# Order of the rounds in a gated delta-rule layer of a decoder kernel

## The reference

```python
q = jax.nn.silu(_dwconv_causal(x @ Wq, qconv_w, qconv_b))      # k and v in the same way
alpha, beta = jax.nn.sigmoid(x @ Wa + ba), jax.nn.sigmoid(x @ Wb + bb)
def step(S, inp):
    qt, kt, vt, at, bt = inp
    err = jnp.einsum('bhvk,bhk->bhv', S, kt) - vt
    S = at[..., None, None] * S - bt[..., None, None] * err[..., :, None] * kt[..., None, :]
    return (S, jnp.einsum('bhvk,bhk->bhv', S, qt))
_, outs = jax.lax.scan(step, S0, (qT, kT, vT, aT, bT))
o = (o - mu) * jax.lax.rsqrt(var + EPS) * ln_g + ln_b          # per head, over 128 values
o = (o * jax.nn.sigmoid(x @ Wg)).reshape(Bx, Lx, NH * DV)
return o @ Wo
...
x = _layernorm(x + _L0_attn_ref(x, ...), axis=-1)
```

## Time and profile before

| | us |
|---|---|
| median of three runs | 3799.28 (3796.48 to 3801.1) |
| the profiled execution | 3798.25 |
| its span in the profile | 3796.5 |
| PE busy, whole span | 3257.8 (86%) |
| DVE busy, whole span | 2811.0 (74%) |
| ACT busy, whole span | 1990.9 (52%) |
| POOL busy, whole span | 1132.7 (30%) |

### The profile page before, as it was taken

How to read it: one execution, slowest core, us unless ns; L and a number is a source line. 1 busy time by engine, 2 the same in 40 slices (tenths; PEclk the granted TensorE clock), 3 DMA queues, 4 the chain that set the end, 5 groups by cost and what they waited for, 6 DMA issues and landing times. The chain is left out here.

```text
span 3796.5 us, 63508 instructions
## 1 busy us (share of the span) xinstructions
PE 3257.8 (86%) x22659; PEld 2092.0 (55%) x22674; DVE 2811.0 (74%) x5796; ACT 1990.9 (52%) x4818; POOL 1132.7 (30%) x1191
## 2 busy tenths in 40 slices
PE   7899999998871777879899978789999999997775
PEld 3466666666551445655566645555666666664444
DVE  6888888886458675553477857769888898985768
ACT  5577777776632333321344425436666566663555
POOL 2633332264003000000011212106666565653210
PEclk9999999999995898889899979999999999997988
DMA  3433333332101100001000000312222222222000
GB/s 104 105 88 96 87 87 91 83 88 54 49 16 33 37 1 25 2 28 38 23 1 1 1 34 2 127 42 69 81 71 78 73 78 73 76 76 73 2 1 23
DMA packets 245463, 200.88 MB, mean 53 GB/s; under 512 B 114720, under 2 KB 213408, under 8 KB 244256
## 3 DMA queue, kind: packets, MB, share of 16 engines
q1 hardware_dynamic: 245152, 196.82, 17.5%
HBM read 181.39 MB, written 15.34 MB: 52 GB/s over the span
## 5 line engine op out<-in xcount | busy, mean ns | idle before, releaser
L310 PE MATMUL ps<-xT,min 128*128 128x512 f32 (+1 forms) x1072 | 496.1, 608 | 11.9 <-DVE macc L3475 11.4
L3475 DVE SCALAR_TENSOR_TENSOR macc<-ps,mcw,macc 128x508 f32<-128x508 f32 (+2 forms) x408 | 302.6, 742 | 80.0 <-ACT macc L3402 70.4
L3576 POOL TENSOR_TENSOR mSQ<-mSQ,mtn 128x512 f32<-128x512 f32 x128 | 234.9, 1835 | 331.1 <-ACT mtn L3427 331.0
L310 PEld LDWEIGHTS ps<-xT,min 128*128 128x128 f32 (+1 forms) x1072 | 191.0, 189 | 228.2 <-issue 205.7
L3569 POOL TENSOR_TENSOR mE<-mE,mCB 128x1024 f32<-128x1024 f32 x128 | 302.0, 2360 | 44.4 <-DVE mE L3485 26.4
L3485 DVE TENSOR_TENSOR_SCAN mE<-mE,mid 128x1024 f32<-128x1024 f32 x128 | 300.1, 2345 | 0.0
L3335 PE MATMUL ps<-mwo,macc 128*128 128x256 f32 x1024 | 243.0, 380 | 5.4 <-DVE macc L3492 5.4
L3080 DVE TENSOR_REDUCE hMX<-ps 128x2 f32<-128x512 f32 x256 | 165.4, 686 | 109.7 <-PE ps L2967 109.0
L3423 ACT ACTIVATE mtn<-ps,mcol 128x64 f32<-128x64 f32 x1024 | 222.1, 333 | 2.8 <-PE ps L3314 2.8
L3047 ACT ACTIVATE hE<-ps 128x512 f32<-128x512 f32 x256 | 138.9, 595 | 156.4 <-PE ps L2961 156.4
L2961 PE MATMUL ps<-hXE,hKE 32*128 32x256 f32 x1024 | 158.9, 428 | 54.8 <-DVE hMX L3080 40.7
(11 more groups left out here) (583 smaller groups left out, 8179.2 us busy)
## 6 DMA issues: line engine op xcount, KB each, us to landing
mE<-m_decay SPq DMA_DIRECT2D x128, 512.0 KB, 3.6
dE<-d_decay SPq DMA_DIRECT2D x64, 264.0 KB, 3.4
dwk<-in_L_attn_Wk SPq DMA_DIRECT2D x64, 128.0 KB, 2.3
dwq<-in_L_attn_Wq SPq DMA_DIRECT2D x64, 128.0 KB, 2.4
dwv<-in_L_attn_Wv SPq DMA_DIRECT2D x64, 128.0 KB, 2.3
dwg<-in_L_attn_Wg SPq DMA_DIRECT2D x64, 128.0 KB, 2.3
dwo<-in_L_attn_Wo SPq DMA_DIRECT2D x64, 128.0 KB, 2.3
min<-in_m_in SPq DMA_DIRECT2D x2, 4096.0 KB, 18.4
```

The lines of the kernel that those rows point to most:

```text
L310: t = pe.matmul(out, w[:, j, :], self.c.xT[:, j, blk(g, 512)], start=j == 0, stop=j == 1)
L3475: x = dve.scalar_tensor_tensor(out=acc[:, :, 3 - j:T], in0=p[:, :, 0:T - 3 + j], scalar=self.cw[:, i, j:j + 1], in1=acc[:, :, 3 - j:T], op ...
L3576: pool.tensor_tensor(self.SQ[g % 2][:, :], self.SQ[g % 2][:, :], self.tn[s][:, :], ALU.add).then_inc(*self.sqa.up)
```

## The change

Four things are changed in `order`, with what follows from them.

1. From round 64 on, v of unit w + 1 stands ahead of vt (behind p32) and no longer behind p64. In rounds up to 63 it keeps its place.
2. o stands directly behind gate, ahead of v1 and e, and oc, which was the first step of the next round, stands behind o in the same round.
3. acc is given unit x - 1 in place of x: each output projection comes one round later, and behind o. dGO becomes two tiles in turn, go waits for acc of unit u - 2, and SP loads the output weights one round later. close moves with acc.
4. The norm of a group, which was one step (stats) in the round after close, with scale in the second round after and turn in the third, becomes six rounds: close, then stat0 and stat1 (mean and variance of two sequences each), root0 and root1 (the root's first Newton step, then two more), scale, and turn behind it.

```diff
--- before.py
+++ after.py
@@ -61,6 +61,10 @@
 
 def blk(j, n=128):
     return slice(n * j, n * j + n)
+
+
+def blk2(j):
+    return 2 * j, 2 * j + 1
 
 
 class Core:
@@ -352,12 +356,12 @@
             for e in range(2):
                 sp.dma_start(self.bia[blk(g, 32), e:e + 1], i["d_abb"][blk(e, 32)]).then_inc(small, 16)
         sp.dma_start(self.small[:, :], i["d_small"]).then_inc(small, 16)
-        for t in range(-4, self.U + self.LAG + 4):
+        for t in range(-4, self.U + self.LAG + 5):
             if t == 0:
                 self.decays_out(sp)
                 for u in range(4):
                     self.decay_in(sp, u)
-            a, b, v, w, x = t + 4, t + 1 - self.LAG, t + 2 - self.LAG, t - 1 - self.LAG, t - 2 - self.LAG
+            a, b, v, w, x = t + 4, t + 1 - self.LAG, t + 2 - self.LAG, t - 1 - self.LAG, t - 3 - self.LAG
             if 0 <= a < self.U:
                 if a >= 4:
                     sp.wait_ge(*self.qp.at(a - 3))
@@ -453,7 +457,7 @@
         self.ak, self.aq, self.av = (c.f32("d" + n, 512) for n in ("ak", "aq", "av"))
         self.KQ, self.E, self.V, self.W = c.sets(2, "dKQ", 4, 2, 128), c.sets(4, "dE", 4, 132), c.f32("dV", 512), c.f32("dW", 512)
         self.seed = c.sets(2, "dsd", 4, 132)
-        self.G, self.O, self.L, self.GO = c.sets(2, "dG", 512), c.sets(3, "dO", 512), c.f32("dL", 512), c.f32("dGO", 512)
+        self.G, self.O, self.L, self.GO = c.sets(2, "dG", 512), c.sets(3, "dO", 512), c.f32("dL", 512), c.sets(2, "dGO", 512)
         self.TT, self.T, self.X, self.X2 = c.sets(4, "dTT", 512), c.sets(4, "dT", 4, 64), c.sets(2, "dX", 4, 32), c.sets(2, "dXX", 4, 64)
         self.s8, self.sw = c.sets(2, "dst", 8, 8), c.sets(2, "dsw", 24)
         self.NB, self.TB, self.TTB, self.tmp = c.sets(2, "dNB", 32, 32), c.f32("dTB", 32, 32), c.f32("dTTB", 32, 32), c.f32("dtmp", 256)
@@ -480,14 +484,16 @@
     def order(self):
 
 
-        for t in range(self.U + self.LAG + 8):
+        for t in range(self.U + self.LAG + 12):
             a, b, v, w, x = t, t - 1, t - self.LAG, t - self.LAG - 2, t - self.LAG - 5
-            every = (("oc", w - 1), ("k", a), ("st", w - 1), ("c1", w - 1), ("c2", w - 2), ("p32", v), ("k1", a), ("on", x), ("q", a), ("vt", w),
-                     ("cols", a), ("s0", b), ("s1", b), ("k2", a), ("p64", v - 1), ("q1", a), ("seed", a), ("v", w + 1), ("ot", x), ("v0", w + 1),
-                     ("go", x), ("w", w), ("q2", a), ("gate", x + 1), ("v1", w + 1), ("e", a), ("acc", x), ("v2", w + 1), ("o", w),
-                     ("close", x), ("stats", x - 1), ("scale", x - 2), ("turn", x - 3))
+            y, late = w + 1, t >= self.U
+            every = (("k", a), ("st", w - 1), ("c1", w - 1), ("c2", w - 2), ("p32", v), ("k1", a), ("on", x), ("q", a), *([("v", y)] * late),
+                     ("vt", w), ("cols", a), ("s0", b), ("s1", b), ("k2", a), ("p64", v - 1), ("q1", a), ("seed", a), *([("v", y)] * (not late)),
+                     ("ot", x), ("v0", y), ("go", x), ("w", w), ("q2", a), ("gate", x + 1), ("o", w), ("oc", w), ("v1", y), ("e", a),
+                     ("acc", x - 1), ("v2", y), ("close", x - 1), ("stat0", x - 2), ("stat1", x - 3), ("root0", x - 4), ("root1", x - 5),
+                     ("scale", x - 6), ("turn", x - 7))
             for step, u in every:
-                if step in ("close", "stats", "scale", "turn"):
+                if step in ("close", "stat0", "stat1", "root0", "root1", "scale", "turn"):
                     due = u % 16 == 15 and (step, u) != ("turn", self.U - 1)
                 elif step in ("c1", "c2"):
                     due = u % 2 == 1
@@ -624,7 +630,7 @@
                     for b in range(2):
                         pe.wait_ge(*room[b])
                 for j in range(4):
-                    t = pe.matmul(bank(j // 2)[:, blk(j % 2, 256)], self.GO[:, blk(j)], self.wo[u % 4][:, :],
+                    t = pe.matmul(bank(j // 2)[:, blk(j % 2, 256)], self.GO[s][:, blk(j)], self.wo[u % 4][:, :],
                                   start=h == 0 and j % 2 == 0, stop=h == 15 and j % 2 == 1, skip_group_check=True)
                 t.then_inc(*self.accd.up)
                 if h == 15:
@@ -831,9 +837,9 @@
             elif step == "go":
                 dve.wait_ge(*self.os.at(u + 1))
                 dve.wait_ge(*self.gt.at(u + 1))
-                if u:
-                    dve.wait_ge(*self.accd.at(u))
-                dve.scalar_tensor_tensor(out=self.GO[:, :], in0=self.G[s][:, :], scalar=1.0, in1=self.L[:, :],
+                if u >= 2:
+                    dve.wait_ge(*self.accd.at(u - 1))
+                dve.scalar_tensor_tensor(out=self.GO[s][:, :], in0=self.G[s][:, :], scalar=1.0, in1=self.L[:, :],
                                          op0=ALU.add, op1=ALU.mult).then_inc(*self.go.up)
             elif step == "close":
                 dve.wait_ge(*self.accd.at(u + 1))
@@ -843,9 +849,25 @@
                 for j in range(4):
                     x = dve.tensor_tensor(c.R[:, j, :], bank(j // 2)[:, blk(j % 2, 256)], c.X[:, 4 * g + j, :], ALU.add)
                 x.then_inc(*self.summed.up)
-            elif step == "stats":
+            elif step in ("stat0", "stat1"):
                 dve.wait_ge(*self.summed.at(g + 1))
-                last = c.moments(dve, own, [(c.R[:, j, :], 0) for j in range(4)], c.st, c.rsq, 1e-5)
+                for j in blk2(int(step[4])):
+                    last = own(dve.bn_stats(c.st[:, j, 0:6], c.R[:, j, :]))
+                dve.wait_ge(own.sem, last)
+                for j in blk2(int(step[4])):
+                    last = own(dve.bn_aggr(c.st[:, j, 6:8], c.st[:, j, 0:6]))
+            elif step == "root0":
+                y, v, a = (c.rsq[:, blk(i, 4)] for i in range(3))
+                dve.wait_ge(own.sem, last)
+                then(dve.tensor_scalar(v, c.st[:, :, 7:8].rearrange("p a b -> p (a b)"), 1e-5, None, ALU.add))
+                then(dve.tensor_scalar(y.bitcast(I32), v.bitcast(I32), 1, None, ALU.logical_shift_right))
+                then(dve.tensor_scalar(y.bitcast(I32), y.bitcast(I32), -1.0, 1597463007.0, ALU.mult, ALU.add))
+                last = self.newton(dve, own, y, v, a)
+            elif step == "root1":
+                y, v, a = (c.rsq[:, blk(i, 4)] for i in range(3))
+                for _ in range(2):
+                    dve.wait_ge(own.sem, last)
+                    last = self.newton(dve, own, y, v, a)
             elif step == "scale":
                 dve.wait_ge(own.sem, last)
                 c.scale_vector(dve, g, c.R)
```

## The result

The changed kernel takes 3769.8 us (median of four runs, 3763.52 to 3771.71) against 3799.16 before (four runs, 3796.48 to 3801.1): a ratio of 0.992, 95% interval 0.9909 to 0.9932. The profiled execution took 3769.95 us with a span of 3768.2. The last closing add of the block starts at 1035.01 us and not at 1063.99; what follows it is 2733.15 us long (2732.47 before). So in the profiled executions the whole gain, 28.98 us, lies in the block.

The account below looks back on a forecast made before the run. PE's own work bounds full rounds; PE idles at group norms, in late rounds and in the tail. Gains 10.2 + 2 + 10.9 + 5.4 - 0.4 = 28.1 us gave 3770 us, range 3759 to 3784.

Parts of the forecast that it names:

- Full rounds: Rounds with PE always busy: only order changes, a round stays at 14.47 us, o never waits for dW; cost 0.
- Rival D: Full rounds: dW comes late for o, PE waits each round, kernel ends slower, 3810 us at 0.8 a round; chance 0.05.
- Norms of groups 0 and 1: Divided norm pieces fit DVE's idle time at round ends, so PE's stalls there mostly vanish: 10.2 us gained.
- Rival B: Norm pieces do not fit beside GpSimd or the taps; half the stall returns, 3777 to 3784 us; chance 0.18.
- the rule of the shared port: Norm pieces: two-SBUF-input VectorE and GpSimd instructions take turns; a piece meeting a batch's start grows by up to 1.95 us.
- Short stalls: Nine PE waits at v or gate as GpSimd batches start, 412 to 838 us: most vanish, 2 us gained.
- Late rounds: Rounds 65 to 76: earlier values and roots bring rounds to 10.22 and 10.39 us; 10.9 us gained.
- the sign that I had named: Late rounds: no 1.85 us wait of on for DVE's roots should remain.
- Tail: After round 76: PE's 3.98 us wait for on falls to 2.3, the clock stays up; 5.4 us gained.
- Rival C: Late rounds stay near 11 us because ACT carries them; 8 us fewer gained, 3779 us; chance 0.08.

Follow-up runs that it names:

- the last kernel: Changed kernel with c2 ahead of st and, in late rounds, acc ahead of w and the values' silu ahead of the copy dO: 3760.23 us, ratio 0.9903.
- slow roots: Changed kernel with ten extra 128x8 products on DVE ahead of the roots in round 78 alone: 3771.44 us, ratio 0.9928.

## Why the prediction was right

3770 was forecast, 3769.8 measured. That the two agree to 0.2 us is luck: single executions of the changed kernel lie 8 us apart, and two terms that came out larger than forecast were cancelled by a stretch that took longer for no reason in the change. What the forecast had right is the mechanism and the size of most terms. The terms, by the table and the rows above:

- **Full rounds, 0.** Right: 14.47, o never idle in them after round 26. Rival D, the slower one, is out: dW's copy ends at 376.04 and o starts at 376.53.
- **Norms of groups 0 and 1, 10.2.** Measured 5.1 + 4.8 = 9.9, and 11.2 with the division alone. Rival B is out in full rounds. Which part of group 1's gain belongs to the division is blurred: o's move alone took 3.3 of it. A part of each 5.5 us that the forecast did not name was the clock: behind the wait of 3.80 us the value projection took 2.79 us where 1.98 is usual, at a granted clock of 0.50 from 448 to 450, and in the changed kernel it was 1.00 from 446 to 450. The row L818 that I put beside the rule of the shared port reads one tile (dst) and not two. It took as long as GpSimd's instruction beside it (1.95 and 1.99 us), but the row with two tiles is the go of 2.12 us above.
- **Short stalls, 2.** They gave 0.9 + 0.8 + 2.2 = 3.9 us (26 to 34, 41 to 50, 57 to 64), twice the forecast. The run with o's move shows the same, the run with the norm alone most of the last and nothing of the others, so the others come with the move of o, oc and acc. The start to round 26 took 2.6 us more than before, and hides that. It is not the change: the kernel before and those with the norm or the values alone have the same list there, and took 306.8, 310.6 and 309.2 us. Its cause was not tested.
- **Late rounds, 10.9.** 11.0 by the windows, but not put together quite as forecast: the plain rounds took 10.23, even ones too, where I had 10.39 for these, and round 70 alone cost 3.8, where I had spread 3.2 over three rounds. In it on still waited 2.15 us, against the sign that I had named. The mechanism (roots late behind dO, ACT's list pacing the rest) is what the runs with c2, o and the values alone show from three sides.
- **Tail, 5.4.** 6.1 by the windows. The wait was forecast as 2.3 (2.26), the clock's fall as gone. The wait follows from the list; that the clock did not fall behind it was in part luck, since behind 2.26 and 2.27 us it fell in two other kernels.
- Rival C (ACT holds the late rounds near 11) is out: the plain rounds took 10.23, and 9.28 was reached in the last kernel with the same work on ACT.

The parts do not add up. Alone, norm, o and values gave 12.1, 18.1 and 0.3 us, some 30 together against the 29.4 of the change. That the sums are near each other hides that the values gave nothing alone, where the clock's falls ate the shorter odd rounds, and some 3 on top of the rest, of which a part is again the clock.

## What to carry to other kernels

Ask of every step in a hand-written list what it waits for and whether what stands behind it needs that. Here c2 needed nothing of this round, stood behind a step that waited, and held up ACT and with it PE every second late round; moving it past the wait brought 18 us alone. Work that is spread out to fit in idle time must also miss the rounds in which a short chain on that engine is awaited: 1.4 us of DVE ahead of an even round went with 4 us more there, and ahead of an odd one with none.

## What the runs showed of the hardware

TensorE's clock fell in places where no single wait was long. It stayed at 2.4 GHz in the changed kernel behind 2.26 us of idle PE (round 78, gate 1.88 us), and fell to 1.2 GHz in round 70 behind 2.03 and 0.77 us (gate 3.32), and in the values-only kernel behind 1.59 and 0.78 us (gate 2.81). Waits that stand near each other do not explain it either: in round 70 of that same kernel the clock stayed behind 1.83 and 0.78 us. Nor does the length of one wait alone: in round 78 it fell in two kernels of five behind 2.25 to 2.27 us, and in all four behind 3.98 to 4.26. I had argued from single waits; these rows do not show what else decides, and a forecast should give such a fall a chance and a price. A fall cost 1.5 to 3 us here (1.6 in round 78 with slow roots, 2.9 in the tail before). The page "TensorE: Matmul & The Clock Gate" of the Trainium skill (section "What's actually happening") gives the two levels and the fall after idling; the rows agree on both.

VectorE's small steps take longer beside GpSimd's work, by different amounts. In round 70 one 128x8 product took 0.57 us and not 0.17, while the same engine's three taps, which read PSUM, kept their 2.29 to 2.30 us.
